# Gathered rows added to z inside PSUM by identity products, one TensorE signal per group, six z banks and six row buffers

## The chip, the cores and the metric

The kernel runs on one core of one Trainium2 chip. Its time is the device time of one execution in microseconds (us); the median of three runs before the change is 2730.47 us (2729.11 to 2732.34). The data are fp32 throughout, with int32 index lists.

The core has five engines that work side by side and wait for one another through counters called semaphores: TensorE (matrix products, written to PSUM; "PE" in the profile, and "PEld" for the loading of its stationary operand), VectorE ("DVE"), ScalarE ("ACT"), GpSimd ("POOL") and SyncE ("SP", which here only issues DMAs). PSUM has eight banks of 128 partitions by 512 fp32 numbers.

## The reference

The work is one layer of a graph network on 12500 nodes with 64 features and 200000 edges with 41 features; the edges come sorted by destination node.

```python
total_edge = jnp.concatenate([node_feats[src], node_feats[dst], edge_feats], axis=-1)
nbr_filter = jax.nn.sigmoid(_bn(total_edge @ W1.T + b1, g1, bt1))
nbr_core = jax.nn.softplus(_bn(nbr_filter, g2, bt2))
h = nbr_filter * nbr_core
agg = jax.ops.segment_sum(h, dst, num_segments=N_NODES)
new_node = _bn(agg, g3, bt3)
return node_feats + new_node
# and around it: x = _layernorm(x + layer(x, ...))
```

`_bn` normalises every feature over all edges (or nodes), so no value can pass it before the whole of its input has been seen. That divides the kernel into stages.

## The kernel before

**Stages.** The first stage (to about 2250 us of the span) computes z = total_edge @ W1.T + b1 for all edges, stores it to HBM and gathers its statistics. The change is in this stage alone. Later stages read z back, apply the two normalisations, sum by destination and finish the nodes.

**Tiling of the first stage.** Edges come in 195 full groups of 1024 and one ragged group of 320. A group is two halves of 512 edges; z of a group is a tile of 128 partitions (64 features of half 0, 64 of half 1) by 512 columns (edges). Two groups make a pair; a pair shares one load of edge features and one load of destination indices. z of a group is a sum of two parts:

- *Destination part and edge part.* Since edges are sorted, the destinations of a half lie within 76 rows of a small table `q_table` (x @ W_dst). `make_hot` (line 691, VectorE) writes a one-hot matrix of the destinations into `into_z`, whose lower rows hold the edge features and a row of ones; `window` (line 467, TensorE, instruction at line 471) multiplies it by `with_w`, which holds the 76 rows of `q_table` and the weights of the edge features: two products, one for each half. The result goes to one of two PSUM banks `z_ps`.
- *Source part.* For the first eight groups ("x groups") GpSimd gathers rows of x, TensorE turns them (`turn_x`, line 435), ScalarE copies them to `xg`, and a product with `w_rows` is added in PSUM (line 502). From group 8 on GpSimd gathers rows of `p_table` (x @ W_src), eight indirect DMAs of 128 rows for each group (`gather`, line 389, instruction at line 400), into one of four buffers `rows` of 128 x 4 x 128. The rows come with edges on partitions, so TensorE turns them: four transposes for a group (`turn`, line 439, instruction at line 447) into one of four PSUM banks (`xg_ps` and `q_ps`).

**How z is put together.** ScalarE copies `z_ps` to `z_sb` (`copy_z`, line 574). VectorE then adds the turned rows from PSUM to `z_sb` (line 724), takes the statistics of the tile (line 726) and, after every second group, writes `near_one` for the later stage (line 689). ScalarE issues the store of a pair (line 578) and the load of a `q_table` window for each group (line 588).

**Signals.** TensorE raises two semaphores for each group from 8 on: `e_ready` after the products of `window`, for which `copy_z` waits, and `turned` after the four transposes, for which VectorE's add and GpSimd's next gather into the same buffer wait.

**What sets the order.** Each engine has one queue, written out by hand; the loops run over groups (TensorE, VectorE, GpSimd) or over pairs and fours (SyncE, ScalarE).

- GpSimd: gather after gather. `gather(g)` into a buffer that group g - 4 used waits until `turned` says that group g - 4 has been turned.
- TensorE: z of group g, then turn of group g (for groups 8 to 18 the turn goes some groups ahead). z of g waits for ScalarE's copy of g - 2 (two banks), for the pair's load, both `q_table` windows and the one-hot. The turn of g waits for the gathered rows and for VectorE's add of g - 4 (four banks).
- SyncE: `load` (line 336) for a pair j: destination indices (after the one-hots of pair j - 1), store of `near_one` of pair j - 2 (line 314), then a wait for the copy of group 2j - 3, then the edge features (line 346) and two `q_table` windows (line 349).
- VectorE in `group(g)`: one-hot of g + 2, add of g, statistics of g, `near_one` if g is odd.

## Time and profile before

| | before |
|---|---|
| median of 3 runs | 2730.47 us (2729.11 to 2732.34) |
| the profiled execution | 2747.09 us |
| its span, first to last instruction | 2745.2 us |
| busy: PE / DVE / ACT / POOL | 886.9 / 1030.1 / 550.1 / 1737.1 us |
| mean granted TensorE clock | 0.596 of full speed |
| last gather issued in the first stage | 2233 us from the span's start |
| first work of the second stage | 2252.6 us |

Busy time is the time in which an engine has an instruction in work; waiting, branching and issuing of hardware DMAs don't count. "Idle before" is the time for which an engine had no work ahead of an instruction, and the name behind the arrow is what ended that time: an engine and a line, a DMA, "issue" where the profile shows nothing that was waited for, and "remote" where a semaphore changed at that moment but the profile can't pair the change with an instruction that had just ended. In a timeline the first number is the start, the second the duration (or the extent of "xN" instructions merged into the row), both in us.

### The profile page before, as it was taken

Reading aid. Unit: us, or ns where it says so; the run is one execution under the profiler, and the core shown is the slowest. Engines: PE = TensorE matmul, PEld = TensorE weight load, DVE = VectorE, ACT = ScalarE, POOL = GpSimd, SP = SyncE. Lnnn points to the kernel's source line nnn. Section 1 sums busy time; section 2 is a strip of 40 time slices with the busy share of each in tenths; the row PEclk is TensorE's granted clock in tenths of the full one; section 3 lists DMA queues with packets and bytes.
Section 4 is the critical chain, followed back from the end, with each engine's and each line's share of the span. In section 5 each row is a group of like instructions: output and inputs, shape, how many; then the busy total and the mean of one; then the engine's idle time right before and its main releaser. Section 6 shows DMA issues by size and latency. Waiting matters only on the chain. (4 is left out here: it accounts for less than half of the span.)

```text
span 2745.2 us, 20113 instructions
## 1 busy us (share of the span) xinstructions
PE 886.9 (32%) x5714; PEld 447.2 (16%) x5714; DVE 1030.1 (38%) x1548; ACT 550.1 (20%) x530; POOL 1737.1 (63%) x1674
## 2 busy tenths in 40 slices
PE   2433222222222232223222321232222310177776
PEld 1211101000000010001000100010001100167662
DVE  2223312222222222222222222122212339899997
ACT  0100000000000000000000000000000029799974
POOL 7466667666766766667666766676667631287763
PEclk7665555555555555555555555555555555599998
DMA  5455535443443444345433544466655439888952
GB/s 150 125 139 154 143 79 123 120 111 87 122 120 95 114 129 120 89 101 130 120 97 98 125 119 102 99 175 178 166 150 129 120 124 384 317 303 298 296 150 95
DMA packets 247389, 404.66 MB, mean 147 GB/s; under 512 B 66782, under 2 KB 132124, under 8 KB 234736
## 3 DMA queue, kind: packets, MB, share of 16 engines
q1 hardware_dynamic: 141417, 290.49, 35.8%
q0 software_dynamic: 50048, 51.30, 10.0%
q10 hardware_dynamic: 55819, 61.63, 6.7%
q8 instruction: 46, 0.75, 0.1%
q14 instruction: 59, 0.48, 0.1%
HBM read 295.52 MB, written 107.76 MB: 147 GB/s over the span
## 5 line engine op out<-in xcount | busy, mean ns | idle before, releaser
L400 POOL DMA_INDIRECT rows<-p_table,src_idx x1496 | 1411.3, 943 | 724.6 <-issue 441.6
L471 PE MATMUL z_ps<-into_z,with_w 128*64 128x512 f32 (+1 forms) x784 | 373.7, 1051 | 1070.9 <-issue 909.2
L574 ACT ACTIVATE z_sb<-z_ps 128x512 f32<-128x512 f32 x196 | 115.6, 596 | 2008.8 <-remote 1320.1
L724 DVE TENSOR_TENSOR z_sb<-z_sb,xg_ps 128x512 f32<-128x512 f32 x141 | 96.2, 682 | 950.4 <-remote 565.3
L696 DVE TENSOR_TENSOR into_z<-d_in,node_ps 84x1024 f32<-84x1024 f32 x196 | 235.5, 1202 | 190.1 <-DMA d_in<-dst_f 118.8
L447 PE MATMUL xg_ps<-ident,rows 128*128 128x128 f32 x564 | 155.1, 429 | 340.9 <-DMA rows<-p_table,src_idx 218.0
L1016 POOL TENSOR_TENSOR h_buf<-h_buf,s_all 128x1536 f32<-128x1536 f32 x66 | 223.5, 3431 | 59.3 <-ACT h_buf L987 59.3
L471 PEld LDWEIGHTS z_ps<-into_z,with_w 128*64 128x64 f32 x784 | 59.1, 202 | 1148.1 <-issue 1094.8
L447 PEld LDWEIGHTS xg_ps<-ident,rows 128*128 128x128 f32 x564 | 100.1, 215 | 563.8 <-DMA rows<-p_table,src_idx 302.4
L724 DVE TENSOR_TENSOR z_sb<-z_sb,q_ps 128x512 f32<-128x512 f32 (+1 forms) x47 | 31.7, 675 | 378.1 <-remote 335.1
L726 DVE BATCH_NORM_STATS2 stats<-z_sb 128x512 f32 (+1 forms) x196 | 135.7, 692 | 52.8 <-DVEq L721 18.7
L1027 PE MATMUL sum_ps<-near,h_rows 128*64 128x84 f32 x3128 | 128.2, 238 | 66.7 <-DVE agg L1081 66.0
L1027 PEld LDWEIGHTS sum_ps<-near,h_rows 128*64 128x64 f32 x3128 | 119.0, 137 | 80.4 <-issue 50.5
L1088 DVE COPY h_rows<-turn_ps 128x1536 f32<-128x1536 f32 x65 | 113.6, 1748 | 7.9 <-PE turn_ps L1037 7.9
L979 ACT ACTIVATE h_buf<-s_all,bn 128x1536 f32<-128x1536 f32 x66 | 108.1, 1639 | 2.9 <-PEq L767 2.8
L1037 PE MATMUL turn_ps<-ident,h_buf 128*128 128x128 f32 (+1 forms) x782 | 101.7, 281 | 9.8 <-POOL h_buf L1016 9.8
L1081 DVE TENSOR_TENSOR agg<-agg,sum_ps 64x84 f32 x392 | 93.6, 239 | 13.8 <-PE sum_ps L1027 3.1
L987 ACT ACTIVATE h_buf<-h_buf 128x1536 f32<-128x1536 f32 x66 | 97.0, 1469 | 2.1
L447 PE MATMUL q_ps<-ident,rows 128*128 128x128 f32 x186 | 51.3, 430 | 135.7 <-DMA rows<-p_table,src_idx 119.1
L1037 PEld LDWEIGHTS turn_ps<-ident,h_buf 128*128 128x128 f32 (+1 forms) x782 | 85.8, 143 | 16.5 <-POOL h_buf L1016 10.3
L867 DVE BATCH_NORM_STATS2 stats<-s_all 128x6 f32<-128x512 f32 x147 | 87.3, 680 | 0.0
L689 DVE TENSOR_TENSOR near_one<-node_ps,rel 128x672 f32<-128x672 f32 x98 | 82.0, 837 | 0.0
(149 smaller groups left out, 721.5 us busy)
## 6 DMA issues: line engine op xcount, KB each, us to landing
s_all<-edge_mem SPq DMA_DIRECT2D x102, 768.0 KB, 7.3
d_in<-dst_f SPq DMA_DIRECT2D x97, 672.0 KB
edge_mem<-z_sb ACTq DMA_DIRECT2D x97, 512.0 KB
into_z<-e_main SPq DMA_DIRECT2D x98, 336.0 KB
near<-near_mem SPq DMA_DIRECT2D x65, 504.0 KB, 4.6
near_mem<-near_one SPq DMA_DIRECT2D x97, 336.0 KB
rows<-p_table,src_idx POOLq DMA_INDIRECT x1496
agg<-edge_mem SPq DMA_DIRECT2D x8, 768.0 KB
```

What stands on the lines that cost most here:

```text
L400: gp.indirect_dma_start(out=to[0:size.tile, t, h, :], out_offset=None, in_=table, in_offset=bass.IndirectOffsetOnAxis(ap=which, axis=0)).t ...
L447: mm = pe.transpose(xg_ps[s][:, t * size.tile:(t + 1) * size.tile], rows[s][0:size.tile, t, :, :].rearrange("p h f -> p (h f)"), ident[0:s ...
L471: mm = pe.matmul(to[h * F:(h + 1) * F, 0:w], which(h)[0:height], into_z[s][0:height, h, 0:w], start=first, stop=last)
L574: act.activation(z_sb[s][:, 0:size.half], z_ps[s % 2][:, 0:size.half], ACT.Copy).then_inc(e_copied, 1)
L696: v.tensor_tensor(hot[s][:, :, 0:size.half], d_in[:, s % 2, :, 0:size.half], node_col[0:WIN, bass.ds(g * 2, 2)].rearrange("p (h a) -> p h ...
L724: v.tensor_tensor(z, z, xg_ps[s][:, part], ALU.add).then_inc(z_copied, 1)
L726: v.bn_stats(stats[:, bass.ds(g, 1), :].rearrange("p a k -> p (a k)"), z_sb[s][:, 0:size.half]).then_inc(z_counted, 1)
L979: act.activation(m.cols(h_buf[m.slot % H]), m.cols(s_in[m.slot]), ACT.Exp, scale=bn2[:, 0:1], bias=bn2[:, 1:2]).then_inc(raised, 1)
L1016: gp.tensor_tensor(m.cols(h_buf[m.slot % H]), m.cols(h_buf[m.slot % H]), m.cols(s_in[m.slot]), ALU.mult).then_inc(h_ready, 1)
L1027: mm = pe.matmul(sum_of(k, h), h_rows[m.slot % 2][0:n.tile, k, t, h * F:(h + 1) * F], hots[0:n.tile, h * n.tiles + t, :], start=(t == 0), ...
L1037: mm = pe.transpose(turn_ps[m.slot % 2][0:m.size.tile, k, t, :], h_buf[m.slot % H][:, k, t * m.size.tile:(t + 1) * m.size.tile], ident[:])
L1088: v.tensor_copy(h_rows[m.slot % 2][:], turn_ps[m.slot % 2][:]).then_inc(rows_ready, 1)
```

## The change

Buffers: rows in three pairs (six buffers) in place of four; z in three pairs of PSUM banks (six) in place of two; the four banks of turned rows are gone. A few small tensors move into memory that lies free (`base_all`, `reach_row`, `dst_ri`, `dst_rrf`). TensorE's turn from group 8 on is an ordinary product with the identity that adds to the z bank, VectorE's add is gone, and TensorE raises one semaphore, `z_ready`, for each group.

```diff
-            rows = [sb(f"rows{s}", [P, TILES, 2, F]) for s in range(S)]
+            R_PAIRS = 3
+            rows_of_pair = [[sb(f"rows{r}_{k}", [P, TILES, 2, F]) for k in range(2)] for r in range(R_PAIRS)]
...
-            z_ps = [stage.enter_context(nc.psum_tensor(f"z_ps{s}", [P, HALF], F32)) for s in range(2)]
-            xg_ps = [stage.enter_context(nc.psum_tensor(f"xg_ps{s}", [P, HALF], F32)) for s in range(3)]
+            Z_PAIRS = 3
+            z_ps = [[stage.enter_context(nc.psum_tensor(f"z_ps{n}_{k}", [P, HALF], F32)) for k in range(2)] for n in range(Z_PAIRS)]
+            spare_ps = stage.enter_context(nc.psum_tensor("spare_ps", [P, HALF], F32))
...
                     if not isinstance(j, int) or j >= 2:
                         store_near(j - 2, s)
-                        sp.wait_ge(e_copied, j * 2 - 2)
+                        sp.wait_ge(z_copied, j * 2 - 2)
...
                 def gather(g, size, table):
-                    s = g % S
-                    if g >= 2 * S:
-                        gp.wait_ge(turned, g - (2 * S if g < 3 * S else S) + 1)
+                    p = g // 2
+                    if X_PAIRS <= p < X_PAIRS + R_PAIRS:
+                        gp.wait_ge(turned, g - X_GROUPS + 1)
+                    elif p >= X_PAIRS + R_PAIRS:
+                        gp.wait_ge(z_ready, g - 2 * R_PAIRS + 1)
...
-                def turn(g, s, turns, size):
-                    pe.wait_ge(gathered[s], lists * 2 * TILES * 16 + 2 * size.tiles * 16)
...
-                        pe.wait_ge(z_copied, g - S + 1)
+                def turn(to, rows, size):
                     for t in range(size.tiles):
-                        mm = pe.transpose(xg_ps[s][:, t * size.tile:(t + 1) * size.tile],
-                                          rows[s][0:size.tile, t, :, :].rearrange("p h f -> p (h f)"), ident[0:size.tile, 0:size.tile])
-                    mm.then_inc(turned, 1)
+                        mm = pe.matmul(to[:, t * size.tile:(t + 1) * size.tile],
+                                       rows[0:size.tile, t, :, :].rearrange("p h f -> p (h f)"), ident[0:size.tile, 0:size.tile],
+                                       start=False, stop=t == size.tiles - 1)
+                    return mm
...
-                    after(pe, e_copied, g - 1)
...
-                        window(to, s, w, lambda h: with_w[s][:, h, :], P, True, alone).then_inc(e_ready if alone else win_used, 1)
+                        window(to, s, w, lambda h: with_w[s][:, h, :], P, True, False)
...
+                def x_pair(p, general):
+                    if p in TURN_BEFORE_PAIR:
+                        turn_x(TURN_BEFORE_PAIR[p])
+                    if p == Z_PAIRS - 1:
+                        pe.wait_ge(xg_ready, X_GROUPS)
+                    after(pe, z_copied, 2 * (p - Z_PAIRS) + 2)
+                    to = z_ps[p % Z_PAIRS]
+                    for k in range(2):
+                        g = 2 * p + k
+                        z_of(g, g % S, g // S, FULL, to[k], general)
                         pe.wait_ge(xg_ready, g + 1)
-                        pe.matmul(to[:, 0:w], w_rows, xg[g][:, 0:w], start=False, stop=True).then_inc(e_ready, 1)
+                        pe.matmul(to[k][:], w_rows, xg[g][:], start=False, stop=True).then_inc(z_ready, 1)
+
+                def p_pair(p, n, turn_of_s, turn_of_r, sizes, general):
+                    to, r = z_ps[n % Z_PAIRS], (n - X_PAIRS) % R_PAIRS
+                    pe.wait_ge(z_copied, (p - Z_PAIRS) * 2 + 2)
+                    for k in range(2):
+                        z_of(p * 2 + k, (n % 2) * 2 + k, turn_of_s, sizes[k], to[k], general)
+                        pe.wait_ge(gathered[2 * r + k], turn_of_r * 2 * TILES * 16 + 2 * sizes[k].tiles * 16)
+                        turn(to[k], rows_of_pair[r][k], sizes[k]).then_inc(z_ready, 1)
...
                 def copy_z(g, s, turn, size):
-                    act.wait_ge(e_ready, g + 1)
+                    act.wait_ge(z_ready, g + 1)
...
-                        if s % 2 == 0 and not (isinstance(i, int) and g < 2):
-                            store_pair(i * 2 + s // 2 - 1, (s // 2 - 1) % 2)
+                        if s % 2 == 1:
+                            store_pair(g // 2, s // 2)
...
                 def group(g, s, turn, size, general):
-                    lead = 1 if general else 2
...
-                    v.wait_ge(e_copied, g + 1)
...
-                        v.wait_ge(turned, g + 1)
-                        v.tensor_tensor(z, z, xg_ps[s][:, part], ALU.add).then_inc(z_copied, 1)
+                    if general:
+                        hot_of(g + 1, s + 1, turn, True)
+                    elif s % 2 == 0:
+                        hot_of(g + 2, s + 2, turn, False)
+                        hot_of(g + 3, s + 3, turn, False)
                     v.wait_ge(z_copied, g + 1)
                     v.bn_stats(stats[:, bass.ds(g, 1), :].rearrange("p a k -> p (a k)"), z_sb[s][:, 0:size.half]).then_inc(z_counted, 1)
```

`z_copied` is now raised by ScalarE's copy. `hot_of(g, ...)` calls `make_hot` for group g where there is one. The "general" branch, for destinations spread too widely, isn't taken with these inputs.

## Rows read from the trace of the kernel before

**Rows 1.** Page, part 2: GpSimd's busy share in 40 slices.

```profile
POOL 7466667666766766667666766676667631287763
```

**Rows 2.** View of line 400: durations (min/median/max ns), first and last start, GpSimd's idle (us, times).

```profile
L400 POOL DMA_INDIRECT rows<-p_table,src_idx x1496: 938/944/961, 116.1 to 2222.5; - x187
...
L400 POOL DMA_INDIRECT rows<-p_table,src_idx_r x4: 896/899/908, 2229.4 to 2233.0; - x4
...
  issue: 461.7, 1514
  remote: 216.4, 39
  PE xg_ps L447: 43.9, 9
  DMA p_table<-s_all: 28.6, 1
```

**Rows 3.** Timeline of GpSimd, 1040 to 1070 us: ends and starts of three gathers.

```profile
1044.59 0.94 POOL L400 DMA_INDIRECT rows<-p_table,src_idx  x1 [0.30 <-issue]
1045.84 0.94 POOL L400 DMA_INDIRECT rows<-p_table,src_idx  x1 [0.30 <-issue]
1052.76 0.94 POOL L400 DMA_INDIRECT rows<-p_table,src_idx  x1 [5.98 <-remote]
...
1061.50 0.94 POOL L400 DMA_INDIRECT rows<-p_table,src_idx  x1 [0.30 <-issue]
1067.57 0.94 POOL L400 DMA_INDIRECT rows<-p_table,src_idx  x1 [5.13 <-PE xg_ps L447]
```

**Rows 4.** Timeline of TensorE, 1004 to 1024 us.

```profile
1009.45 1.98 PE L471 MATMUL z_ps<-into_z,with_w 128*64 128x512 f32 x4
1018.46 1.11 PE L447 MATMUL q_ps<-ident,rows 128*128 128x128 f32 x4 [7.03 <-DMA rows<-p_table,src_idx]
1022.37 1.98 PE L471 MATMUL z_ps<-into_z,with_w 128*64 128x512 f32 x4 [2.81 <-issue]
```

**Rows 5.** Timeline of the other engines, 1040 to 1075 us.

```profile
1042.72 0.60 ACT L574 ACTIVATE z_sb<-z_ps 128x512 f32<-128x512 f32 x1 [20.40 <-remote]
...
1052.59 0.69 DVE L724 TENSOR_TENSOR z_sb<-z_sb,q_ps 128x512 f32<-128x512 f32 x1 [18.35 <-remote]
...
1056.70 4.21 SPq L349 DMA_DIRECT2D with_w<-q_table  x2
1063.05 0.60 ACT L574 ACTIVATE z_sb<-z_ps 128x512 f32<-128x512 f32 x1 [19.73 <-remote]
...
1063.70 1.98 PE L471 MATMUL z_ps<-into_z,with_w 128*64 128x512 f32 x4 [17.31 <-issue]
...
1067.91 0.60 ACT L574 ACTIVATE z_sb<-z_ps 128x512 f32<-128x512 f32 x1
```

**Rows 6.** Views of lines 574 and 724: idle time before ScalarE's copy and VectorE's add.

```profile
  remote: 1320.1, 92
...
  remote: 900.4, 59
```

**Rows 7.** Groups by line, 300 to 2200 us: busy, mean ns of one, idle before.

```profile
L696 DVE TENSOR_TENSOR into_z<-d_in,node_ps 84x1024 f32<-84x1024 f32 x169 | 203.8, 1206 | 153.8 <-DMA d_in<-dst_f 88.0 <-issue 65.8
L724 DVE TENSOR_TENSOR z_sb<-z_sb,xg_ps 128x512 f32<-128x512 f32 x127 | 86.6, 682 | 885.5 <-remote 565.3 <-PE xg_ps L447 212.5 <-issue 107.7
```

**Rows 8.** Timeline, x groups: a 128x512 product that isn't a transpose.

```profile
127.46 2.08 PE L502 MATMUL z_ps<-s_all,w_both 128*128 128x512 f32 x2
```

**Rows 9.** Windows: length, busy of PE, PEld, DVE, ACT, POOL, TensorE clock, DMA share.

```profile
300.00:2200.00 1900.00, 505.25 (x1348) 171.07 (x1348) 488.89 (x596) 99.87 (x169) 1267.72 (x1344) 0.53 0.47 120
```

**Rows 10.** Timeline, end of the first stage: last turn, last add, first work behind it.

```profile
2242.81 0.53 PE L447 MATMUL q_ps<-ident,rows 80*128 80x80 f32 x2
...
2244.63 0.31 DVE L724 TENSOR_TENSOR z_sb<-z_sb,q_ps 128x160 f32<-128x160 f32 x1
...
2252.64 0.10 POOL L844 MEMSET ones_col<- 128x1 f32 x1 [18.70 <-POOLq L177]
```

More of the change, by code:

```diff
@@ L254, in build @@
             q_low, q_high = ([sem(f"{n}{s}") for s in range(S)] for n in ("q_low", "q_high"))
-            gathered = [sem(f"gathered{s}") for s in range(S)]
-            ahead = [sem(f"ahead{s}") for s in range(S)]
+            gathered = [sem(f"gathered{r}") for r in range(2 * R_PAIRS)]
+            x_gathered = [sem(f"x_gathered{g}") for g in range(X_GROUPS)]
             z_stored = [sem(f"z_stored{s}") for s in range(2)]
@@ L472, in window, with z_of @@
                     return mm
[L474 removed]
+                def z_of(g, s, turns, size, to, general):
                     w = size.half
[L476 to L478 removed]
                     if s % 2 == 0:
@@ L504, in all_groups @@
                 def all_groups(general):
+                    for p in range(X_PAIRS):
+                        x_pair(p, general)
+                    LOOP = 2 * Z_PAIRS
                     if general:
-                        for g in range(X_GROUPS):
-                            if TURN_BEFORE_Z.get(g, X_GROUPS) < X_GROUPS:
-                                turn_x(TURN_BEFORE_Z[g])
-                            z_of(g, g % S, g // S, FULL, True)
-                        with pe.Fori(2, R_TURN) as i:
-                            for s in range(S):
-                                z_of(i * S + s, s, i, FULL, True)
-                                turn(i * S + s, s, i, FULL)
@@ L527, in all_groups @@
-                    z_of(GROUPS, R_SLOT, R_TURN, RAGGED, general)
-                    turn(GROUPS, R_SLOT, R_TURN, RAGGED)
+                        for p in range(X_PAIRS, LOOP):
+                            p_pair(p, p, p // 2, (p - X_PAIRS) // R_PAIRS, (FULL, FULL), True)
+                        with pe.Fori(1, (PAIRS_OF - 1) // LOOP) as i:
+                            for n in range(LOOP):
+                                p_pair(i * LOOP + n, n, i * (LOOP // 2) + n // 2, i * (LOOP // R_PAIRS) + (n - X_PAIRS) // R_PAIRS, (FULL, FULL), True)
@@ L529, in all_groups @@
+                    for p in range((PAIRS_OF - 1) // LOOP * LOOP if general else X_PAIRS, PAIRS_OF):
+                        p_pair(p, p, p // 2, (p - X_PAIRS) // R_PAIRS, (FULL, RAGGED if p == PAIRS_OF - 1 else FULL), general)
                     pe.wait_ge(z_copied, GROUPS + 1)
```

106 lines of the change are left out of this document (38 added, 68 removed).

## The prediction

> **What bounds the kernel now.** I read the page first, then the view of GpSimd's gather line, then the timelines of one stretch in the middle of the stage. In the page, GpSimd is the only engine that is more than half busy through the first stage [rows 1]. The view of its line says why: 1496 indirect DMAs of 944 ns each run from 116.1 us on, and the last four begin by 2233.0 [rows 2]. Between two of them lies a gap of 0.30 us, so one costs 1.25 us [rows 3] and a group of eight 9.98 us. That is the floor: 187 groups x 9.98 + 4 x 1.2 = 1872 us. The stretch takes 2233.9 - 116.1 = 2118 us, 246 us more. The same number comes from the waits: 216.4 us over 39 "remote" waits and 43.9 over 9 that end with a turn on line 447, 260.3 together [rows 2]; each of these 48 holds the 0.3 us that is paid anyway, which leaves 246. (The 28.6 us for `p_table` come before 116.1 and stay.) So GpSimd is the bound, and 246 us of the stage are its waits for `turned`: 11.3 us a group instead of 10.
>
> Why is `turned` late? Not for want of TensorE: it works 505 of 1900 us [rows 9]. Counting the instructions along each engine, the products at 1009.45 are z of group 87, the transposes at 1018.46 its turn, the products at 1022.37 z of group 88 [rows 4]. The copy of 87 starts at 1042.72, the add of 87 at 1052.59, the copy of 88 at 1063.05 [rows 5]. ScalarE and VectorE had been idle for 18 to 20 us each time, and the profile calls what released them "remote". So a result that TensorE finished at 1011.4 is announced 31 us later, one of 1019.6 33 us later, one of 1024.4 39 us later. The gather that resumes at 1052.76 waits for just the turn of 87 [rows 3]: two engines saw that semaphore move at the same moment. TensorE's signals come late, one after another: 1042.7, 1052.5, 1063.0, about 10.2 us apart, alternately for z and for a turn. Then, at 1063.70, TensorE runs again, and by 1067.57 everything that was held has come: the turn of 88 [rows 3], and the copy of 90 at 1067.91 [rows 5]. Over the whole stage such "remote" waits stand before 92 copies and 59 adds [rows 6].
>
> So the loop is: two signals a group at about 10 us each, while a group's gather takes 10 us; the lateness grows by some 10 us a group. GpSimd bears it until buffers run out: gather 91 needs the turn of 87, which ended 27 us before the gather could have started (1046.8, rows 3), and came 6 us too late. What causes the late signals no row shows. I take them as a fact of this stage.
>
> **The Trainium skill on signals.** "TensorE: Matmul & The Clock Gate" (section "The cost: per-tile semaphore tail") says that increments serialise at about 26 ns each. By that rule, as an estimate, half of 390 signals would be worth 5 us of TensorE and nothing of GpSimd. The trace disagrees with it as an account of this stage: a signal is 31 to 39 us late [rows 4, 5].
>
> **The change part by part.**
>
> 1. *One signal a group.* The signal after `window` goes, the one after the turn stays. If each costs the 10.2 us between neighbours in rows 5, 20.4 us a group become 10.2, against 9.98 us of gather: the lateness hardly grows. If the spacing were free, I would gain the same, since GpSimd is the floor either way.
> 2. *Six row buffers.* Gather g now waits for the signal of g - 6, not g - 4: two groups, 20 us, more. The lateness that GpSimd bears rises from 27 to 47 us. The largest in rows 4 and 5 is 39. Each stretch with two waits like those of rows 3 (6.0 and 5.1 us) is then covered even if signals stay as late as now. This is the part on which the forecast rests most.
> 3. *Six z banks.* z of g waited for the copy of g - 2: the products at 1063.70 start 0.65 us after the copy at 1063.05 [rows 5], so this wait binds now. It moves back to the pair three pairs before. What is late next is the pair's load on SyncE: it still waits for the copy of group 2j - 3, then issues the edge features and two windows, of which the pair takes 4.2 us to issue [rows 5]; with landing some 9 us. So z of a pair comes no sooner than the signal of 2j - 3 plus 9, and keeps up with the gathers (30 us for three groups) while the lateness is under 21 us.
> 4. *The turn as a product.* Four transposes take 1.11 us [rows 4]. The nearest row of an fp32 product with as many columns (512) and a full stationary operand is 2.08 us [rows 8], at the same low clock. Bounds: 1.1 from below; from above 2.1 plus eight weight loads of 0.2, 3.7. I take 2.1, for the row is the same form. TensorE then has 2.0 + 2.1 a group of 10 us; at 3.7 still 5.7. GpSimd's pace hides it. With that cover gone (at the end of the stage) it costs 1 us once.
> 5. *No add on VectorE.* 188 x 0.68 = 128 us [rows 7] leave an engine that works 489 of 1900 us [rows 9]; it isn't the bound, so nothing directly. It takes one 0.7 us step and one wait for a signal out of the chain to the next one-hot. Between 0 and a few us; I take 0.
> 6. *One-hots for two groups at once.* The same 1.2 us each [rows 7]. The second is made one group sooner; the first before the same wait as now. On VectorE, the statistics of g queue behind 2.4 us of one-hots, if those wait for `d_in` (88 us in all over 1900 [rows 7]). 0, at most 1 us once at the end.
> 7. *Stores.* ScalarE issues a pair's store right behind its own second copy, so waits 0.6 us for itself; behind it are the next copy and window load. Hidden, ScalarE is 5% busy [rows 9].
> 8. *The start.* Gathers 8 to 13 go without any new wait; gather 14 is due at 116.1 + 60 = 176 and waits for z of group 8, which must pass the x groups first. Now some 14 us are lost from 116 to 220 us (they are in the 246). In the new order z must precede the turn, so I don't expect all of it back: between 0 and 20 us, I take 8.
> 9. *The end.* From the last gather's end (2233.9) to the last turn are 9 us, to the next stage 18.7 [rows 2, 10]. Part of the 9 is again a late copy. Between -5 and +10, with the 1 us of step 4; I take +2.
>
> By the Trainium skill, same page, section "Terms", transposing mode is 4 times as fast for fp32 as an ordinary product. Taken on the row of 1.11 us that would be 4.4 us a group, as an estimate; rows 8 say 2.08, and even 4.4 would stay under GpSimd's 10.
>
> Sum, on the profiled execution: 2747.1 - 246 + 8 + 2 = 2511. The median of the runs is 2730.5, 16.6 us below the profiled one; less that, **2495 us** (-8.6%). Moves of 0.2% (5 us) and less can't be told from none in this kernel.
>
> **The rivals.**
>
> - *The signals still set the pace (13%).* If each signal costs 10.2 to 10.7 us whatever precedes it and they are never released together, 187 x 10.5 = 1963 us instead of 1867: +96, **2590 us**. For it: the even spacing in rows 5. Against: the bunch by 1067.57 [rows 3, 5], which would have to stop.
> - *The z side takes over (10%).* The lateness stays above 21 us, the pair's load (step 3) comes late, and with it the turn, which now stands behind z of its own group. GpSimd keeps one wait in two: 246 / 2 = 123 back, **2618 us**. For it: that wait isn't loosened, and z and turn now share one signal. Against: 20 us of lateness lent by the buffers.
> - *Slower: the lateness counts TensorE's instructions, not its signals (12%).* Place: between the end of a turn and `z_ready`. A group has 16 matmuls and weight loads now (8 for z, 8 for the turn), and would have 24, as fp32 products are recorded two for each (x2 in rows 8, one product). The late stretch, some 58 us of each 8 groups, would become 87: +29, less the 20 us that two buffers absorb, less the 11 us now lost, leaves 9 + 11 = 20 us lost in 8 groups instead of 11. That is 12.5 us a group instead of 11.4: 187 x 1.1 = +206, **2936 us**. It decides from the point where the added lateness exceeds what the buffers lend. For it: neither row tells signals from instructions. Against: spacings after z (8 instructions of twice the columns) and after a turn are nearly the same.
> - *No change (3%)*: the gains of the middle are lost in the start or behind VectorE's new order.
>
> **How the numbers follow.** The forecast has 62%, the rivals 13, 10, 12 and 3. The predicted time is the forecast's. Its own range is 2472 to 2525 (steps 8 and 9 at their ends). 23% lie at 2590 to 2620, so the range must reach past them: **2470 to 2640 us**, which leaves out the slower case and no change, about 15%, and 3% below. Faster 62 + 13 + 10 = 85%, the same 3%, slower 12%.
>
> **What would show it.** Right: in the view of the gather line, 1.25 us a DMA as now, "remote" and TensorE waits together under 30 us, the last gather at about 1995 us; groups 10 us apart in any window; the second stage of unchanged length. Step 2 is wrong if waits of 5 us remain before gathers although the last signal is under 47 us late. Step 1 is wrong if the copies are spaced over 10.5 us for long stretches. Step 3 shows in products that start right behind the landing of their loads and not behind the gathered rows. Step 4: a group of turn products over 4 us. The slower rival shows in copies more than 50 us behind their products. The forecast falls altogether if the signals' lateness grows with the work per group, or if another wait fills GpSimd's gaps.

## The result: 1% slower on the first chip, the same on another

The change was predicted to save 235 us. It saved none. Beside each other on one chip, the kernel before took 2729.9 us (median of 4 runs, 2729.11 to 2732.34) and the changed kernel 2759.77 us (4 runs, 2748.49 to 2761.41); ratio 1.0099, 95% interval 1.0071 to 1.0127. The experiments ran on six chips, and there the size of the question changed: on three (7, 9 and 10) the median of the kernel before is 2734 to 2743 us, nearly as here, on the other three (3, 12 and 15) 2465 to 2468 us. On one of the latter the changed kernel took 2468.82 us against 2468.20; ratio 1.0001 (0.9991 to 1.0011). I call the first kind *late* chips and the second *prompt* ones, for reasons that the traces show below. One of the 19 executions of the kernel before on chip 12, a prompt one, took 2765.02 us at a mean granted clock of 1.0, where the other 18 took 2462.82 to 2466.66 at 0.60 to 0.61; it is in no ratio, it has no trace, and it is a reason not to take "late" for a fixed property of a chip.

The profiled execution after took 2748.49 us (span 2746.7), the lowest of its four; the one before took 2747.09, 17 us over its median. So the two traces are nearly equally long, and what they show is where the forecast's saving went, not the 30 us between the medians.

Page, part 2 of the changed kernel: GpSimd's busy share in 40 slices. GpSimd is no busier than in [rows 1].

```profile
POOL 7456666666666666666666666666666641287763
```

View of the gather line after (as [rows 2]):

```profile
L405 POOL DMA_INDIRECT rows<-p_table,src_idx x1496: 938/944/961, 114.8 to 2236.9; - x187
...
L405 POOL DMA_INDIRECT rows<-p_table,src_idx_r x4: 896/902/910, 2238.1 to 2241.7; - x4
...
  remote: 227.9, 46
  PE z_ps L443: 45.2, 10
  DMA p_table<-s_all: 27.7, 1
```

A gather costs what it did. GpSimd's waits for TensorE are 227.9 + 45.2 = 273.1 us in 56 waits, where they were 260.3 in 48 [rows 2]; the last gather starts 8.7 us later. All that was to vanish is still there.

Timeline after, TensorE and ScalarE, 1129 to 1163 us (as [rows 4, 5]):

```profile
1129.03 0.29 PEld L443 LDWEIGHTS z_ps<-ident,rows 128*128 128x128 f32 x1 [2.51 <-issue]
1129.04 0.60 ACT L574 ACTIVATE z_sb<-z_ps 128x512 f32<-128x512 f32 x1 [23.25 <-remote]
...
1130.43 0.37 PE L443 MATMUL z_ps<-ident,rows 128*128 128x128 f32 x1 [2.43 <-issue]
1132.53 0.29 PEld L443 LDWEIGHTS z_ps<-ident,rows 128*128 128x128 f32 x1 [3.21 <-issue]
1133.93 0.37 PE L443 MATMUL z_ps<-ident,rows 128*128 128x128 f32 x1 [3.13 <-issue]
1134.63 0.29 PEld L443 LDWEIGHTS z_ps<-ident,rows 128*128 128x128 f32 x1 [1.81 <-issue]
1136.03 0.37 PE L443 MATMUL z_ps<-ident,rows 128*128 128x128 f32 x1 [1.73 <-issue]
...
1153.56 0.60 ACT L574 ACTIVATE z_sb<-z_ps 128x512 f32<-128x512 f32 x1 [23.92 <-remote]
...
1162.10 0.60 ACT L574 ACTIVATE z_sb<-z_ps 128x512 f32<-128x512 f32 x1 [7.95 <-remote]
...
1162.67 0.33 PEld L468 LDWEIGHTS z_ps<-into_z,with_w 128*64 128x64 f32 x4 [22.86 <-issue]
```

Two things are to be seen. The first two copies are 24.5 us apart with one signal a group (the third, behind a stop of GpSimd, comes after 8.5); before, two signals took about 20.4 [rows 5]. And here TensorE's own records are spread out: from 1129.03 to 1136.03 there are six in 7 us, on average 1.4 us from one to the next, though each takes 0.3 to 0.4. In the rows of before its records looked compact and early [rows 4] while results came late. I read this so: TensorE isn't done and silent; it gets through its queue very slowly, and a record can stand ahead of the work. The records counted in the traces, for the copies of groups 20 to 189, bear it out: between the last product that a copy waits for and the start of that copy, TensorE has never recorded more than 63 further matmuls and weight loads in the changed kernel, and never more than 24 in the kernel before, where two z banks hold it back. 24 records at 1.4 us would be 34 us, an estimate; the late results of [rows 4, 5] are 31 to 39 us late.

### The profile page after: what moved, and what is told of

Its sections match the earlier page's. It is cut to its first block and busy times, and to the rows that moved or that the text cites. A ratio compares the mean times of both kernels' runs of the same rounds, so it can differ in the third digit from the quotient of the medians.

```text
span 2746.7 us, 20944 instructions
## 1 busy us (share of the span) xinstructions
PE 942.0 (34%) x6464; PEld 578.8 (21%) x6464; DVE 903.6 (33%) x1360; ACT 549.5 (20%) x530; POOL 1736.9 (63%) x1674
## 5 line engine op out<-in xcount | busy, mean ns | idle before, releaser
L468 PE MATMUL z_ps<-into_z,with_w 128*64 128x512 f32 (+1 forms) x784 | 321.9, 850 | 1162.0 <-issue 959.7
L443 PE MATMUL z_ps<-ident,rows 128*128 128x128 f32 x1500 | 323.5, 357 | 333.7 <-issue 328.7
L443 PEld LDWEIGHTS z_ps<-ident,rows 128*128 128x128 f32 x1500 | 267.4, 255 | 540.0 <-issue 529.1
L696 DVE TENSOR_TENSOR into_z<-d_in,node_ps 84x1024 f32<-84x1024 f32 x196 | 228.8, 1207 | 234.3 <-issue 130.3
L834 ACT ACTIVATE s_all<-s_all,bn 128x1536 f32<-128x1536 f32 x49 | 79.2, 1660 | 9.7 <-DMA s_all<-edge_mem 9.7
L1071 DVE TENSOR_TENSOR near<-iota_ps,rel 128x1008 f32<-128x1008 f32 x65 | 78.5, 1208 | 2.8 <-DVE iota_ps L1154 0.8
L971 ACT ACTIVATE s_all<-s_all,bn 128x1536 f32<-128x1536 f32 (+1 forms) x38 | 58.9, 1627 | 0.1
```

Of the source, the lines that this page charges most:

```text
L443: mm = pe.matmul(to[:, t * size.tile:(t + 1) * size.tile], rows[0:size.tile, t, :, :].rearrange("p h f -> p (h f)"), ident[0:size.tile, 0: ...
L468: mm = pe.matmul(to[h * F:(h + 1) * F, 0:w], which(h)[0:height], into_z[s][0:height, h, 0:w], start=first, stop=last)
L696: v.tensor_tensor(hot[s][:, :, 0:size.half], d_in[:, s % 2, :, 0:size.half], node_col[0:WIN, bass.ds(g * 2, 2)].rearrange("p (h a) -> p h ...
```

## Experiments

Eight edits of the two kernels, some on several chips. Each ratio is to runs of the kernel before on the same chip. "Records" are TensorE's recorded matmuls and weight loads per group; "waits" are GpSimd's for TensorE in the gather line's view ("remote" plus TensorE).

On late chips (one signal, two signals and four more products ran on chip 7, six row buffers on 9, transposes first on 10; waits and last gathers are from one trace each):

| | records | ratio to before (95%) | waits, us | last gather starts |
|---|---|---|---|---|
| before | 16 | 1 | 260.3 | 2233.0 |
| one signal | 16 | 1.0003 (0.9993 to 1.0012) | 257.0 | 2229.7 |
| six row buffers | 16 | 1.0016 (1.0003 to 1.0029) | 256.8 | 2230.5 |
| transposes first | 16 | 1.0051 (1.0031 to 1.0072) | 257.9 | 2225.1 |
| the change | 24 | 1.0099 (1.0071 to 1.0127) | 273.1 | 2241.7 |
| the change, two signals | 24 | 1.0110 (1.0093 to 1.0127) | 277.5 | 2251.8 |
| the change, four more products | 40 | 1.0186 (1.0169 to 1.0203) | 301.7 | 2270.8 |

On prompt chips every version that does the whole work takes the same: six row buffers 1.0002 (0.9992 to 1.0011), 1.0003 (0.9993 to 1.0012) and 1.0000 (0.9990 to 1.0009) on three chips; transposes first 1.0003 (0.9993 to 1.0013), 1.0003 (0.9993 to 1.0012) and 1.0004 (0.9995 to 1.0014) on the same three; the change 1.0001.

**One signal a group, and nothing else** (step 1).

```diff
-                        window(to, s, w, lambda h: with_w[s][:, h, :], P, True, alone).then_inc(e_ready if alone else win_used, 1)
+                        mm = window(to, s, w, lambda h: with_w[s][:, h, :], P, True, alone)
+                        if g < TURNED_BEFORE:
+                            mm.then_inc(e_ready if alone else win_used, 1)
...
-                    act.wait_ge(e_ready, g + 1)
+                    if isinstance(g, int) and g < TURNED_BEFORE:
+                        act.wait_ge(e_ready, g + 1)
+                    else:
+                        act.wait_ge(turned, g + 1)
```

> The kernel before with one TensorE signal per group (from group 19 on ScalarE's copy of z waits for the signal of the turn; the one after the window products is gone). Instructions, buffers and banks are those of before. If late signals are counted by signals (the forecast's step 1), half of them makes the lateness grow by 10 us a group and not by 20: most of the 246 us of gather waits go, 2500 to 2600 us. If the lateness counts TensorE's instructions, whose number is unchanged (16 recorded per group), it stays at 2730 within 15, with some 260 us of waits before the gathers; a little more is possible because the copy of z, and so the next group's z and load, waits longer.

Measured: 2741.1 us against 2739.8. Half the signals, the same time and the same 257 us of waits.

**A second signal in the changed kernel.**

```diff
+            extra = sem("extra")
...
-                        window(to, s, w, lambda h: with_w[s][:, h, :], P, True, False)
+                        window(to, s, w, lambda h: with_w[s][:, h, :], P, True, False).then_inc(extra, 1)
```

> The changed kernel with a second TensorE signal per group, raised by the window products on a semaphore that nobody waits for. Instruction theory: same as the changed kernel, 2760 within 10. Signal theory: 187 more signals at 10 us each in the stretches in which signals come late; with the cover of the buffers at least 100 us slower, 2860 or more.

Measured: 2768.58 us, ratio 1.0110 where the change alone has 1.0099. 187 more signals cost nothing that can be told from zero. Signals are not what is counted. The Trainium skill ("TensorE: Matmul & The Clock Gate", "The cost: per-tile semaphore tail") would price them, as an estimate, at 26 ns each, 5 us in all, which no run here can tell from nothing either.

**Four more products of 4 columns.**

```diff
+                        if not general:
+                            for t in range(4):
+                                pe.matmul(spare_ps[:, t * 4:t * 4 + 4], ident[:], ident[:, 0:4], start=True, stop=True)
                         turn(to[k], rows_of_pair[r][k], sizes[k]).then_inc(z_ready, 1)
```

> The changed kernel with four more products of 4 columns per group, 16 more recorded instructions (24 to 40) and under 0.5 us of columns, written to a bank that nobody reads; the signals are unchanged. Instruction theory, with 0.70 us per recorded instruction in the late stretches: a group there takes 24 + 11 = 35 us in place of 24, so that GpSimd waits far longer: 2950 to 3400 us. Signal theory, or any theory in which only busy time counts: 2760 to 2770.

Measured: 2790.59 us, waits 301.7. Both theories missed. The new products have 4 columns each, and still the ratio rises from the change's 1.0099 to 1.0186, so instructions do count; but that is 24 us, not 200 to 600. The timeline shows how: one stop of GpSimd, three groups of gathers, one stop again.

```profile
1043.64 0.94 POOL L405 DMA_INDIRECT rows<-p_table,src_idx  x1 [4.58 <-remote]
...
1077.96 0.95 POOL L405 DMA_INDIRECT rows<-p_table,src_idx  x1 [4.62 <-remote]
```

34.3 us for three groups is 11.4 us a group, nearly the 11.3 that the kernel before takes with two stops in eight groups (5.98 and 5.13, [rows 3]). More TensorE instructions make the stops more frequent and shorter; their sum moves from 260.3 to 301.7 us, while the records go from 16 to 40.

**No gathers from group 14 on**, on the same late chip.

```diff
-                for g in range(X_GROUPS, GROUPS):
+                for g in range(X_GROUPS, X_GROUPS + 2 * R_PAIRS):
                     gather(g, FULL, p_table)
-                gather(GROUPS, RAGGED, p_table)
...
-                        pe.wait_ge(gathered[2 * r + k], turn_of_r * 2 * TILES * 16 + 2 * sizes[k].tiles * 16)
+                        pe.wait_ge(gathered[2 * r + k], 2 * TILES * 16)
```

> The changed kernel without the gathers of groups 14 and later: GpSimd is silent from about 180 us on, and TensorE turns old rows (z is then wrong from there on). If late signals belong to TensorE alone (so many instructions, so much time), copies of z stay 20 us and more behind their products, and a group takes the 10 us and more that it takes now. If they come only while GpSimd issues indirect DMAs, each copy follows its last product within 1 us through the whole stage, and the first stage shrinks to what the other engines need, some 6 to 9 us a group (SyncE's and ScalarE's loads): 1600 to 2200 us in all.

Measured: 1505.6 us. What ended ScalarE's idle time before the copies of z:

```profile
L573 ACT ACTIVATE z_sb<-z_ps x196: 305/598/599, 129.7 to 1002.2; 128x512 f32<-128x512 f32 x195, 128x160 f32<-128x160 f32 x1
...
  PE z_ps L442: 703.6, 187
  remote: 32.5, 4
```

Before 187 of the copies it is a turn product that had just ended; "remote" stands before 4, where it stood before 92 [rows 6]. The same TensorE instructions, with the same signals, are prompt when GpSimd gathers nothing, and the stage ends at 1002 us. That is quicker than either theory allowed.

**Six row buffers in the kernel before, and nothing else** (step 2, on which the forecast rested most; the small tensors lie where the change puts them, and each x group has a semaphore of its own). It ran on three prompt chips and one late one.

```diff
-            rows = [sb(f"rows{s}", [P, TILES, 2, F]) for s in range(S)]
+            R = 6
+            rows = [sb(f"rows{r}", [P, TILES, 2, F]) for r in range(R)]
...
-                        gp.wait_ge(turned, g - (2 * S if g < 3 * S else S) + 1)
+                        gp.wait_ge(turned, g - (X_GROUPS if g < X_GROUPS + R else R) + 1)
```

> The kernel before with six row buffers in place of four, nothing else (two z banks, transposes, VectorE's add, two signals per group; the small tensors lie where the change puts them). The forecast's step 2 by itself: GpSimd bears 20 us more of lateness, so most of the 246 us of waits go: about 2500 to 2600 us. Rival A (TensorE runs its instructions slowly in these stretches and the backlog only ends when GpSimd stops for some us): buffers only move the stop, 2740 within 10 on this chip, with fewer but longer waits, adding up to the same 250 us. Rival B (the pace of 11.4 us per group belongs to the gathers themselves): the same 2740.

Measured, on a prompt chip: 2465.11 against 2464.92 for the kernel before. Two more runs:

> The kernel before with six row buffers. On a chip with late signals: by the forecast's step 2, 2500 to 2600 us; if the backlog only ends when GpSimd stops, the same as before, 2735 within 10, with fewer and longer waits. On a chip without them 2465 as measured.

> The kernel before with six row buffers. Where before takes 2735: by the forecast's step 2, 2500 to 2600 us; if the backlog only ends when GpSimd stops, 2735 within 10, with fewer and longer waits. Where before takes 2465: 2465.

Both chips were prompt: 2467.87 and 2464.5 us, before's time. On the late one:

> The kernel before with six row buffers, once more, for a chip with late signals. Where before takes 2735: by the forecast's step 2, 2500 to 2600 us; if the backlog only ends when GpSimd stops, 2735 within 10, with fewer and longer waits. Where before takes 2465: 2465 again.

Measured: 2749.83 against 2743.11.

```profile
L401 POOL DMA_INDIRECT rows<-p_table,src_idx x1496: 938/944/961, 116.0 to 2225.6; - x187
...
  remote: 210.1, 34
  PE xg_ps L444: 46.7, 10
```

The waits sum to 256.8 us. By the timeline they still come in twos, 6.2 and 5.2 us before groups 93 and 94, 5.5 and 5.8 before 101 and 102, eight groups apart as before. What did move is TensorE: gather 93 waits for the turn of 87, six groups back, and that add starts at 1075.4, where before it started at 1052.6 [rows 5]. The two buffers let TensorE fall two groups further behind, once, and then the cycle is the same: from the end of gather 87 to the add of 87 are 56.0 us, where they were 35.8 (1016.8 to 1052.6), 20.2 more for the 20 us that the buffers lend. The gathers end as early as before, but the second stage starts at 2260.4, 29.9 us after the last gather's start, where before it is 19.6.

**The changed kernel beside the kernel before, on a prompt chip.**

> The changed kernel itself, beside the kernel before. On the chip of the last four runs the kernel before took 2465 us, not 2730 to 2740, with no gap in GpSimd's gathers and no late signal; so whether TensorE's signals come late differs from chip to chip. Where before takes 2465, GpSimd's gathers are the floor, one signal or two, four buffers or six, and the change gives 2465 within 8, or some us more for its longer end. Where before takes 2735, the change gives 2760 again.

Measured: 2468.82 against 2468.20.

```profile
L405 POOL DMA_INDIRECT rows<-p_table,src_idx x1496: 940/944/957, 88.6 to 1954.7; - x187
...
L405 POOL DMA_INDIRECT rows<-p_table,src_idx_r x4: 896/901/913, 1956.0 to 1959.6; - x4
its engine sat idle before it (us, times) until:
  issue: 476.1, 1562
  DMA src_idx<-src_t: 2.8, 1
  PE spare_ps L437: 0.3, 1
```

No wait for TensorE but 0.3 us, and none for `p_table` either: 1956.0 - 88.6 = 1867 us for 187 groups, 9.99 a group, the floor that the forecast took. On these chips GpSimd's gathers are the whole stage, before and after.

**Gathers and TensorE side by side, with no wait between them.** From group 14 on GpSimd gathers into a pair of buffers that nobody reads; TensorE turns old rows.

```diff
+                for g in range(X_GROUPS + 2 * R_PAIRS, GROUPS):
+                    k, turn = g % 2, (g - X_GROUPS - 2 * R_PAIRS) // 2
+                    gp.wait_ge(gathered[4 + k], (turn + 1) * 2 * TILES * 16)
+                    for t in range(TILES):
+                        for h in range(2):
+                            gp.indirect_dma_start(out=rows_of_pair[2][k][:, t, h, :], out_offset=None, in_=p_table,
+                                                  in_offset=bass.IndirectOffsetOnAxis(ap=src_idx[:, g, h * TILES + t:h * TILES + t + 1], axis=0)
+                                                  ).then_inc(gathered[4 + k], 16)
...
-                    to, r = z_ps[n % Z_PAIRS], (n - X_PAIRS) % R_PAIRS
+                    to, r = z_ps[n % Z_PAIRS], (n - X_PAIRS) % 2
...
-                        pe.wait_ge(gathered[2 * r + k], turn_of_r * 2 * TILES * 16 + 2 * sizes[k].tiles * 16)
+                        pe.wait_ge(gathered[2 * r + k], 2 * TILES * 16)
```

> The changed kernel, but from group 14 on GpSimd gathers into one pair of buffers that nobody reads and waits only for its own landed gathers, while TensorE turns two pairs of old rows and waits for no gather (z is then wrong from there on): GpSimd and TensorE work side by side without waiting for one another. Theory: late signals come while GpSimd issues indirect DMAs without a stop. Then GpSimd goes on at 10.0 us per group without a gap until about 2010 us, and TensorE falls to the 24 us per group of the late stretches: it has done some 90 groups when GpSimd ends, and does the rest at 6 us a group; the stage ends at 2500 to 2700 us. Rival: the 11.4 us belong to the gathers themselves; then they take 11.4 here too, and TensorE goes ahead of them at 6 us a group and its stage ends with the last gather near 2240.

> Gathers that nobody waits for beside a TensorE that waits for no gather. Without late signals it took 2504 us, the gathers 10.0 us a group and TensorE's side 5 us a group. On a chip with late signals: if GpSimd's gathers make them, the gathers still take 10.0 us a group to 2010 us without a gap, and TensorE falls to 24 us a group from about 180 us until the last gather (some 75 groups), so that the whole takes 2900 to 3200 us; if the lateness needs TensorE to wait for gathered rows, 2504.

> Gathers that nobody waits for beside a TensorE that waits for no gather. Where before takes 2735: if GpSimd's gathers make the signals late, the gathers go on at 10.0 us a group without a gap, TensorE falls to some 24 us a group until the last gather, and the whole takes 2900 to 3200 us; if the lateness needs TensorE to wait for gathered rows, 2504 to 2540. Where before takes 2465: 2504.

Measured: 2504.1, 2504.91 and 2496.34 us, one execution on each of three prompt chips. There TensorE's side is done by 1031 us, and the gathers run on alone.

> Gathers that nobody waits for beside a TensorE that waits for no gather. Where before takes 2740: if GpSimd's gathers make the signals late without any wait between the two, the gathers go on at 10.0 us a group without a gap, TensorE falls to some 24 us a group, and the whole takes 2900 to 3200 us; if the lateness needs the coupling, 2504 to 2540. Where before takes 2465: 2504 again.

Measured, on a late chip, one execution: 3288.34 us (before there: 2734.09). ScalarE on the late chip:

```profile
1000.43 0.60 ACT L581 ACTIVATE z_sb<-z_ps 128x512 f32<-128x512 f32 x1 [33.00 <-remote]
...
1034.04 0.60 ACT L581 ACTIVATE z_sb<-z_ps 128x512 f32<-128x512 f32 x1 [33.00 <-remote]
...
1067.63 0.60 ACT L581 ACTIVATE z_sb<-z_ps 128x512 f32<-128x512 f32 x1 [33.00 <-remote]
...
1101.23 0.60 ACT L581 ACTIVATE z_sb<-z_ps 128x512 f32<-128x512 f32 x1 [33.00 <-remote]
```

A group every 33.6 us, as regular as a clock, from group 7 to group 65: 33.6 / 24 = 1.40 us for each recorded TensorE instruction, be it of a window product with 512 columns or of a turn product with 128. The window 300 to 1000 us of the same kernel on a prompt chip, then on the late one (length, busy of PE, PEld, DVE, ACT, POOL, TensorE clock, DMA share, GB/s):

```profile
300.00:1000.00 700.00, 403.60 (x1684) 212.80 (x1683) 301.12 (x350) 83.58 (x140) 509.39 (x540) 0.77 0.90 246
```

```profile
300.00:1000.00 700.00, 120.32 (x259) 55.07 (x259) 44.00 (x50) 11.94 (x20) 523.42 (x505) 0.51 0.24 53
2220.00:2700.00 480.00, 287.91 (x1270) 154.13 (x1268) 225.54 (x260) 63.28 (x106) 0.00 (x0) 0.79 0.81 248
```

1684 matmuls against 259 in the same 700 us, with GpSimd about as busy and with less DMA traffic, not more (53 GB/s against 246). In the second window of the late chip, where the gathers are over, TensorE does 1270 in 480 us, no less than the prompt chip's pace. GpSimd's last gather starts at 2182.3, and by the timeline TensorE stays slow for some 25 us more: its records are mostly 0.7 to 1.4 us apart from 2189.7 to 2208.6 and come in a burst from there. So on a late chip the gathers alone slow TensorE, with no semaphore between the two.

They suffer too. The gather line on the late chip, then on the prompt one:

```profile
L430 POOL DMA_INDIRECT rows<-p_table,src_idx x1448: 938/947/1942, 174.6 to 2182.3; - x181
```

```profile
L430 POOL DMA_INDIRECT rows<-p_table,src_idx x1448: 938/944/957, 148.1 to 1998.8; - x181
```

That is 11.1 us a group of eight against 10.2, though GpSimd waits for no other engine in either; the mean gather takes 1.036 us against 0.944, with 505 issued in 700 us against 540. From copy to copy 23 to 27 gathers start beside the 24 records of a group (1296 records and 1290 gathers between 300 and 2100 us), about one for one. No run tells why.

The low clock (0.51 of full speed, mostly the 1.2 GHz level, against 0.77) is not the cause: between the two levels lies a factor of two, and the pace differs by 6.5.

**GpSimd busy with memsets in place of gathers.** TensorE's side is that of the run above.

```diff
-                for g in range(X_GROUPS, GROUPS):
+                for g in range(X_GROUPS, X_GROUPS + 2 * R_PAIRS):
                     gather(g, FULL, p_table)
...
-                gather(GROUPS, RAGGED, p_table)
...
+                        gp.memset(rows_of_pair[2][t % 2][:], 0.0).then_inc(made, 1)
```

> As the run with gathers apart from TensorE, but GpSimd writes zeros (memsets of 128x512 numbers, eight for each group, one after another) instead of issuing indirect DMAs; no rows are gathered from group 14 on. If GpSimd's being busy is what slows TensorE, copies of z come 20 us and more behind the products until GpSimd ends. If it is the indirect DMAs, TensorE is as prompt as without gathers, some 6 us a group and a first stage of about 1000 us.

Measured: 1449.45 us, no copy of z behind a "remote". But it ran on a prompt chip, where gathers do no harm either; whether plain GpSimd work slows TensorE on a late chip stays open.

**The change with transposes first.** Four transposes write the z bank, the window products are added to it: everything of the change, but 16 records instead of 24, and the wait for the gathered rows stands ahead of the window products.

```diff
-                                       start=False, stop=t == size.tiles - 1)
+                                       start=t == 0, stop=False, is_transpose=True)
...
-                        window(to, s, w, lambda h: with_w[s][:, h, :], P, True, False)
+                        return window(to, s, w, lambda h: with_w[s][:, h, :], P, first, not first)
```

> The changed kernel with the turn first and as four transposes that write the z bank, and the window products added to it: one signal, six buffers, six banks and no add on VectorE as in the change, but 16 recorded TensorE instructions per group as before, not 24. If TensorE's instructions are what the lateness counts, 8 fewer of 0.7 us (5.6 us a group in the late stretches) bring it below both kernels: 2600 to 2700 us. If the pace is set by GpSimd's having to stop, whatever TensorE does, 2740 to 2770.

Measured, on a prompt chip: 2465.51 against 2464.92. Two more runs:

> Transposes first, window products added, 16 recorded instructions per group in place of 24. On a chip with late signals (before 2735): if 8 fewer instructions matter there, 2600 to 2720 and below both kernels; if the pace is set by GpSimd's having to stop, 2735 to 2765. On a chip without them: 2465 as measured.

> Transposes first, window products added: 16 recorded TensorE instructions per group, one signal, six row buffers, six banks. Where before takes 2735 (late signals): if 8 fewer instructions than in the change matter, 2600 to 2720; if the pace is set by GpSimd's having to stop, 2735 to 2765. Where before takes 2465: 2465.

Prompt chips again: 2468.7 and 2465.7 us. On a late one:

> Transposes first, window products added: the change with 16 recorded TensorE instructions per group in place of 24. Where before takes 2740: six row buffers alone gave 2750 there and one signal alone gave before's time, so I now expect no gain against before, 2740 to 2755, if the change's own 20 to 30 us are the price of its 8 more instructions; if they are the price of its order (pairs, loads), 2760 to 2775. Where before takes 2465: 2465 again.

Measured: 2748.81 against 2734.09. Its waits are back at 257.9 us, like those of every kernel with 16 records (256.8 to 260.3), and its last gather starts at 2225.1. So the change's 13 to 16 us more of waits go with its 8 extra records; with the 40 records of the run above, waits grow by about 1.85 us for each record a group has more ((301.7 - 257.2) / 24, from the mean of the three edits with 16). Its ratio is still 1.0051, and the profiled run shows a part of why: the second stage starts 31.6 us after the last gather's start (at 2256.7), where the kernel before needs 19.6 and the change 14.3, while the rest of the kernel takes 492.3 us against 492.6. So 12 us are lost between the last gather and the second stage, and 8 gained ahead of it, against a trace of before that is itself 17 us over its median. With six row buffers alone the same stretch is 10 us longer. That the backlog that the buffers allow is paid back there is a reading, not shown; the change's own 14.3 show that it isn't so in every trace.

No version that does the whole work beats the kernel before, on the chips on which it was run.

## Why the prediction was wrong

**What failed first** is the fact taken on trust ahead of step 1: "TensorE's signals come late, one after another". TensorE was read as finished because its records stood early and compact [rows 4]. By the runs it wasn't: on a late chip with gathers that never stop it needs 1.40 us for each recorded instruction, and its records stand up to 24 records ahead of a copy in the kernel before, up to 63 in the change. The even 10.2 us between signals would then be 8 records at about 1.3 us, for z as for a turn, which is why the two spacings looked alike.

**Step 1 (one signal)** is wrong: 1.0003 alone, and 1.0110 against 1.0099 when the second signal is put back. With one signal a group the copies of late stretches are 19 to 22.5 us apart in the kernel before and 21 to 29 in the change, the text's own sign against this step (over 10.5).

**Step 2 (six row buffers)**, which carried most of the 246 us, is wrong: 1.0016 alone. The error is one of kind. A buffer lends time once; it pays only if the lateness ends by itself before it is used up. In the traces it doesn't. Six buffers moved TensorE two groups further back and left the stops as they were; the waits stayed between 257 and 302 us in seven kernels with four or six buffers, one or two signals, two or six z banks. Its own sign came true in the change: 6.9 us of wait before gather 94, for a turn whose product was recorded as ended at 1062.8 and whose copy came at 1097.7, 35 us later and not over 47. What buffers have to cover is the time from the end of a gather to its use, 63 us there (1034.6 to 1097.7), in which TensorE hasn't even recorded the turn for the first 26. In the rows the held work comes out only once GpSimd has stopped again (stop at 1062.4, burst by 1067.57, [rows 3]), so a sum that removes the stops removes what ends the lateness. In the run without any stop the copies stay 33.6 us apart for 58 groups, until the gathers end, and then come in a burst. That a stop of 5 to 6 us is enough to cause the burst, and is not only its companion, is argued from these rows; no kernel with stops put in on purpose was run.

**Step 3 (six z banks)** was not run by itself; nothing that can be seen hung on it. TensorE's waits for the landing of the edge features (`into_z<-e_main`, view of the window products) grew from 98.1 us in 13 to 155.8 in 20, as the step foresaw of the pair's load.

**Step 4 (turn as product)** was sized right in time, where its records stand close together: 1.16 to 2.08 us a group where 2.1 was taken:

```profile
1164.61 2.05 PE L443 MATMUL z_ps<-ident,rows 128*128 128x128 f32 x8
...
1167.60 1.16 PE L443 MATMUL z_ps<-ident,rows 128*128 128x128 f32 x8
```

but costed at nothing because GpSimd's 10 us would hide it. What it adds is eight records (x8 matmuls where [rows 4] has x4, and as many weight loads), and with them came 13 to 16 us of waits on a late chip, where GpSimd's pace didn't hide them. On a prompt chip it does (1.0001).

**Steps 5 to 7** (no add, one-hots in twos, stores) were forecast to cost and bring nothing; nothing in the traces speaks against it, but no run sets them apart.

**Step 8 (start)** was put too low, inside its bounds: gather 14 alone waits 19.28 us, where 8 was taken and 20 was the upper bound. The old kernel's waits before 220 us are 5.3, 3.2 and 4.4 us (12.9, where the text says 14), so the start got 6 us longer, where 8 for 14 would have made it 6 shorter.

```profile
193.63 0.94 POOL L405 DMA_INDIRECT rows<-p_table,src_idx  x1 [19.28 <-PE z_ps L443]
```

**Step 9 (end)**: from the last gather's end (2242.6) to the second stage (2256.02) are 13.4 us where there were 18.7 [rows 10]; 5.3 less, at the lower end of its bounds.

**The range.** With steps 8 and 9 at their ends the forecast's own range comes to 2480 to 2515 us; the text has 2472 to 2525. No other number hangs on it. "No change", which came nearest to what was measured, had 3%.

**The rivals.** "Lateness counts TensorE's instructions" was nearest to the mechanism (12%): records, not signals, and slower. Its price was off by a factor of more than 7, some 27 us (0.99%) where it gave 206, and its sign (copies more than 50 us behind their products) didn't show: the largest is 47.9. It let the late stretches grow by the added work and GpSimd wait for all of it; in the runs the stops clear the backlog of records (the copy of 91 before and the copy of 86 in the change start 0.04 us after their product's record), so more work makes the cycle shorter (three groups with 40 records, eight with 16), at nearly the same loss per group. In its sum the 11 us that the words take off are added (9 + 11). "Signals still set the pace" fell with step 1. "The z side takes over" isn't borne out as a rate: the waits aren't halved.

**The floor** holds on prompt chips. Taking out all waits gave 2495 us; chips without lateness take 2465 to 2468, before and after. Span less GpSimd's waits over 0.6 us (the one for `p_table` among them) is 2745.2 - 289 = 2456 before, 2746.7 - 300 = 2447 after, and 2464.5 on the prompt chip, which has none. For a late chip the floor isn't shown: in the one run there in which GpSimd waits for no other engine, a group of gathers takes 11.1 us and not 9.98, and 187 x 11.1 would be 2076 us (an estimate), 42 less than the 2118 of the kernel before and not 246. So even a change that took out every wait might have gained little there.

**What stays open:** whether lateness belongs to the chip or to the time at which it was used, for all runs on one of the six stand close together in time; what a gather takes from TensorE (it slows by the instruction and not by the column, but no row shows why); whether the recording of a profile has a part in it, for every execution here comes with a span and a clock of the profiler, and the slowness is counted by the recorded instruction; and what lets the backlog go.

## What to carry to other kernels

When a result is used long after its producer's record ends, and "remote" is all that the profile says, don't take the record as the end of the work: count what lies in the producer's queue, and test with a kernel that lets the two engines run without a wait between them. A buffer lends its time only once unless the lateness that it covers ends by itself; before summing up waits as a saving, ask what ends the lateness now, and whether the wait is it. And time the kernel before on more than one chip before explaining its waits: here a tenth of its time was there on three chips and not on three others.

## What the runs showed of the hardware

- The same program takes 2465 to 2468 us (medians) on chips 3, 12 and 15 and 2734 to 2743 us on chips 7, 9 and 10, within 0.35% on each but for the one execution of 2765.02 us on chip 12.
- On the late chips TensorE needs 1.40 us for each recorded matmul or weight load while GpSimd issues indirect DMAs without a stop (33.6 us for 24, chip 10), with 512 columns as with 128; once the gathers are over it does 1270 matmuls in 480 us there, against 1684 in 700 on a prompt chip. Without gathers its results are prompt (chip 7, 1505.6 us in all).
- There the gathers suffer too when they never stop: 844 of 1448 still take 0.94 to 0.95 us, but 535 take 1.05 to 1.12 and 51 take 1.93 to 1.94.
- TensorE's records can stand up to 47.9 us ahead of their effect in the changed kernel, and never over 63 records: group 93's last product is recorded as ending at 1114.2, and its copy starts at 1153.56.
- Transposing passes can open a PSUM sum onto which fp32 products are then added, without any cost against the ordinary order (1.0003 on prompt chips).
